# One transformer block: gate columns in place of gate rows, norms applied on ScalarE, a new order of stages

## The chip, the cores and the metric

The kernel runs on one core of one Trainium2 chip. The metric is the device time of one launch in microseconds (us), as the median of several runs. A core has five engines that run side by side and each work through their own instructions in order: TensorE (PE, matmuls), VectorE (DVE), ScalarE (ACT), GpSimd (POOL) and SyncE (SP), which here issues nearly all DMAs. They meet only through semaphores.

## The reference

The input `x` is 2 x 1024 x 512 in float32. A conditioning vector `c` (2 x 512) gives six modulation vectors of 512 per batch; two of them, `ga` and `gb`, are gates, clamped away from zero:

```python
mod = (_silu(c) @ wmod).reshape(2, 6, 1, -1)
sa, ca, ga, sb, cb, gb = ...
ga = (2 * (ga >= 0) - 1) * maximum(abs(ga), 0.25)      # gb the same
h = _layernorm(x) * (1 + ca) + sa
x = x + ga * attn(h)
h = _layernorm(x) * (1 + cb) + sb
x = x + gb * ffn(h)
```

`attn` is a convolution over time with 3 taps (512 to 3 x 128), projections to 16 heads of 64, causal attention within blocks of 128 positions, an output projection to 128 (`wo`) and one to 512 (`proj_w`). `ffn` is a base matmul 512 x 512 plus a low-rank part of rank 64 whose second factor is mixed from 16 experts, of which a softmax router picks two per position.

## The kernel before, in words

**Tiling.** The 2048 positions are worked in 8 chunks of 256 (index `j`), each as two blocks of 128 positions on the partitions (index `b`); `j` 0 to 3 is batch 0. Every float32 operand of the large matmuls is held as a high and a low half in float16, and a product is three matmuls (high x high, high x low, low x high; `PASSES`, `passes`). The halves are made in pairs of operations: ScalarE writes the high half, VectorE (sometimes GpSimd) subtracts and writes the low half. So nearly each result of TensorE passes ScalarE and then VectorE before TensorE can use it again and before its PSUM bank is free. There are three banks `C` (convolution, projections, `pr`, `lr`), one `W` (`pv`, `wo`), two `F` (ffn) and two `S` (scores).

**Order.** The text `SCHEDULE` (L64) lists stages as `name:j:n`. It is expanded to `ORDER` (L108), and each of the five engines loops over the same `ORDER` and issues its own part of each stage, with its waits. So the text fixes the order on every engine at once, but not the times: an engine is held only by its semaphores. `c:j:n` stands for the next `n` of the 108 convolution matmuls of chunk `j` (three thirds q, k, v, of 36), which are spread between other stages as filling.

**Stages that matter here.**
- `na` / `nb`: the first norm. VectorE computes mean and variance (L797), GpSimd forms 1/sqrt in a linked chain of six small operations (`root`, L538), VectorE then applies `(x - mean) * rstd` in place in `xa` (L805). `l2a` / `l2b` are the same for the second norm (L939, L949), from `xb` or `xa` to `xn2`.
- `hs` (L645, L810, L553): the high and low half of the normed chunk; SP turns them with two transposing DMAs into `hT` (L409), and issues the first loads behind them. `halo` (L557) copies the columns at chunk borders. `hs2`: the same for the second norm.
- `row` (L1040, L814): matmuls with the weights `wmod` give the modulation vectors as rows, each repeated over 32 partitions (`QUAD`); `row:0:0` is sa and ca, `row:0:2` is ga (made twice, for 64 partitions), `row:0:3` is sb, cb and gb. VectorE copies them out of PSUM; for `n` 2 and 3 it also clamps the gate, in four linked operations on whole rows of 512 (`clamp`, L777).
- `cols` (L1056, L825): TensorE transposes the rows of scale and shift to columns, VectorE stores them (`modT`, `shift`). The scale goes into the weights, in the splits `sp` (L639, L866); the shift goes through `vb` (convolution bias `cbias`), `fbias` and `lb`.
- `pick` (L1096, L852): one matmul against a selecting column spreads a gate row (or the ffn bias row) over all 128 partitions; VectorE copies it to `gaB`, `gbB` or `gbBB`.
- `pj` (L689, L871, L567): `proj_w` times the gate, split in halves: VectorE multiplies, ScalarE writes the high half, VectorE waits for it and writes the low half.
- `qk`, `v`, `s`, `m`, `e`, `nz`, `ph`, `pv`, `wo`, `pr`: projections, scores, row maxima, exponentials, normalization (GpSimd, L581), halves and transposes of the probabilities, values, output projections and residual. `lr`, `ro`, `rw`, `G`, `gh`, `fb`, `fl`, `gbb`, `xr`: the router, the ffn, its bias and the stores.

Of the kernel before, what the change touches and what calls it, by code (L numbers as in the profile page):

```python
# [42 lines left out]
def bass_adaln_block(nc, x, cw_in, pw_in, wo_in, pj_in, bsw_in, btw_in, ar_in, small_in, pb_in, bb_in, wmod_in,  # L43
# [26 lines left out]
        c:1:15 e:0:2 nz:0:2 c:1:3 cols:0:1 v:0:1 qk:1:0 pv:0:0 s:0:3 qk:1:5 m:0:3 ph:0:2 pick:0:2 qk:1:4 qk:1:1  # L70
        pv:0:1 c:1:3 sp:0:10 c:1:9 e:0:3 c:1:6 nz:0:3 c:1:12 pick:0:3 c:1:3 qk:1:6 v:0:3 c:1:3 hs:3:0 s:1:0 m:1:0
        halo:3:0 fbias:0:0 ph:0:3 qk:1:2 v:1:0 c:2:3 sp:0:7 c:2:6 e:1:0 c:2:3 nz:1:0 c:2:9 pick:0:4 pv:0:2 c:2:3
        qk:1:3 c:2:12 qk:1:7 s:1:1 m:1:1 ph:1:0 pv:0:3 pick:0:5 v:1:1 c:2:9 sp:0:9 c:2:6 e:1:1 c:2:3 nz:1:1 c:2:6
        qk:2:1 wo:0:0 c:2:3 s:1:2 c:2:6 m:1:2 c:2:3 pr:0:1 ph:1:1 pr:0:0 v:1:2 l2a:0:0 qk:2:5 qk:2:0 c:2:3 e:1:2
        c:2:6 nb:4:0 c:2:12 nz:1:2 c:2:3 l2b:0:0 c:2:9 pv:1:0 v:1:3 c:2:3 lb:0:0 s:1:3 hs2:0:0 hs:4:0 na:5:0 v:2:0
        v:2:1 m:1:3 qk:2:4 qk:2:3 xr:1:0 ph:1:2 qk:2:6 pv:1:1 lb:0:1 qk:2:2 lr:0:0 c:3:12 halo:4:0 c:3:3 e:1:3 c:3:3
        nz:1:3 c:3:6 s:2:0 ro:0:0 c:3:6 m:2:0 rw:0:0 ph:1:3 pv:1:2 qk:2:7 c:3:18 e:2:0 c:3:9 nb:5:0 c:3:6 nz:2:0
        c:3:6 ra:0:0 c:3:3 v:2:2 v:2:3 s:2:1 m:2:1 qk:3:1 ph:2:0 c:3:6 G:0:0 pv:1:3 c:3:3 sp:0:11 e:2:1 nz:2:1 c:3:9
# [1220 lines left out]
```

## Time and profile before

| | |
|---|---|
| median of 3 runs | 470.56 us (470.47 to 470.79) |
| the profiled execution's own time | 470.41 us |
| its span, first to last instruction | 468.4 us |
| mean granted TensorE clock | 0.984 |
| TensorE busy | 420.9 us (90%) |
| VectorE busy | 356.3 us (76%) |
| ScalarE busy | 302.0 us (64%) |
| GpSimd busy | 268.8 us (57%) |

All later times are of the profiled execution, counted from the start of its span. An engine's busy time leaves out its waits. In the rows further down, `L808` is line 808 of the kernel, `128x512 f16<-128x512 f32` is what an operation writes and reads (partitions x elements), `x16` a count, and a bracket `[6.92 <-DVE cv L886]` says how long the engine was idle before the instruction and whose end released it. A float32 matmul appears as two records in the trace.

### The profile page before, as it was taken

What the parts mean: (1) busy time and instruction counts of PE and PEld (TensorE: products, weight loads), DVE (VectorE), ACT (ScalarE), POOL (GpSimd) and SP (SyncE); (2) the same over time, 40 slices, a digit from 0 to 9 for tenths busy, and PEclk for the clock granted to TensorE, in tenths of its full rate; (3) what the DMA queues carried; (4) which work ended last, traced back from release to release, by engine and by line L of the source; (5) the groups of instructions that cost most, each with busy time, mean ns of one, the idle gap of its engine ahead of it and who ended that gap; (6) DMA issues with size and microseconds to landing.
All of it is one profiled execution on the core that took longest, in us unless ns stands there. A gap on an engine that the chain in (4) does not pass through costs nothing.

```text
span 468.4 us, 11145 instructions
## 1 busy us (share of the span) xinstructions
PE 420.9 (90%) x4170; PEld 270.2 (58%) x4170; DVE 356.3 (76%) x675; ACT 302.0 (64%) x974; POOL 268.8 (57%) x309
## 2 busy tenths in 40 slices
...
GB/s 318 235 397 388 207 206 46 59 123 47 80 147 113 158 133 202 143 84 115 181 72 157 163 49 145 111 139 117 156 115 46 47 136 90 153 142 45 136 80 77
DMA packets 144901, 65.09 MB, mean 139 GB/s; under 512 B 134704, under 2 KB 134960, under 8 KB 144464
## 3 DMA queue, kind: packets, MB, share of 16 engines
...
q8 instruction: 33, 0.54, 0.5%
q14 instruction: 20, 0.16, 0.1%
...
## 4 chain that ended last, share of the span: by engine, by line
PE 51%; DVE 16%; POOL 10%; DMA 9%; ACT 6%; issue 5%; SPq 2%; ACTq 0%; POOLq 0%; DVEq 0%
PE F L1024 15%; PE C L1133 12%; PE C L1024 10%; PE W L1024 3%; PE S L1179 3%; PE W L1196 3%; ACT prob L705 3%; DMA xa<-in_x_dram 3%; POOL prob L584 2%; DVE p L915 2%; DMA gT<-g 2%; PE S L1024 2%; DMA xb<-in_x_dram 2%; DVE nm L909 2%; DVE qk L895 2%
## 5 line engine op out<-in xcount | busy, mean ns | idle before, releaser
L1133 PE MATMUL C<-hT,cw 128*128 128x256 f16 x864 | 108.4, 277 | 13.0 <-DVE cv L886 6.9
L584 POOL TENSOR_TENSOR prob<-prob,rinv 128x1024 f32<-128x1024 f32 x32 | 62.4, 1948 | 73.7 <-DVE rinv L920 73.7
L1133 PEld LDWEIGHTS C<-hT,cw 128*128 128x128 f16 x864 | 83.0, 99 | 32.1 <-issue 7.4
L705 ACT ACTIVATE prob<-S,nms 128x128 f32<-128x128 f32 x256 | 89.9, 377 | 7.1 <-DVE p L915 6.0
L1024 PE MATMUL F<-btw,gT 128*128 128x512 f16 x336 | 74.8, 379 | 2.2 <-DMA gT<-g 2.1
L676 ACT ACTIVATE qk<-C,bqk 128x256 f16<-128x256 f32 x128 | 52.6, 479 | 14.2 <-PE C L1024 13.4
L895 DVE SCALAR_TENSOR_TENSOR qk<-C,bqk,qk 128x256 f16<-128x256 f32 x128 | 54.3, 474 | 4.6 <-ACT qk L676 4.6
L1024 PEld LDWEIGHTS F<-btw,gT 128*128 128x128 f16 x336 | 32.5, 98 | 40.7 <-DMA gT<-g 2.9
L705 ACT ACTIVATION_READ_ACCUMULATOR prob<-S,nms 128x1 f32 x256 | 55.5, 217 | 0.0
L1024 PE MATMUL C<-cv,pw 128*128 128x256 f16 x384 | 50.4, 273 | 2.4 <-DVE cv L886 1.9
L915 DVE SCALAR_TENSOR_TENSOR p<-prob,p 128x1024 f16<-128x1024 f32 x32 | 48.3, 1509 | 4.6 <-ACT p L714 4.3
L714 ACT ACTIVATE p<-prob 128x1024 f16<-128x1024 f32 x32 | 33.8, 1056 | 22.6 <-POOL prob L584 17.9
L909 DVE TENSOR_REDUCE nm<-S 128x4 f32<-128x512 f32 x64 | 41.0, 682 | 5.5 <-PE S L1179 5.4
L1024 PEld LDWEIGHTS C<-cv,pw 128*128 128x128 f16 x384 | 35.6, 98 | 13.1 <-DVE cv L886 3.4
L1024 PE MATMUL F<-bsw,h 128*128 128x512 f16 x168 | 38.4, 379 | 0.9 <-DVE ob L1014 0.9
L622 POOL TENSOR_TENSOR G<-cmb,lr 128x1024 f32<-128x1024 f32 x15 | 30.6, 2043 | 7.9 <-DVE cmb L998 4.0
L1196 PE MATMUL W<-pt,v 128*64 128x128 f16 x768 | 27.5, 221 | 4.4 <-issue 3.0
L1196 PEld LDWEIGHTS W<-pt,v 128*64 128x64 f16 x768 | 22.5, 110 | 14.3 <-issue 12.4
L1007 DVE TENSOR_TENSOR g<-G,g 128x1024 f16<-128x1024 f32 x15 | 24.2, 1613 | 6.9 <-ACT g L760 6.9
L540 POOL TENSOR_SCALAR rs<-mv 128x2 f32<-128x2 f32 x16 | 8.0, 500 | 34.7 <-DVE mv L803 18.4
L1179 PE MATMUL S<-qk 64*128 64x128 f16 x768 | 27.6, 220 | 0.0
L1024 PE MATMUL C<-pw,cv 128*128 128x512 f16 x96 | 25.0, 380 | 2.0 <-DVE cv L886 2.0
...
## 6 DMA issues: line engine op xcount, KB each, us to landing
...
wmb<-in_wmod_dram SPq DMA_DIRECT2D x1, 3072.0 KB, 19.1
...
```

The lines of the kernel that those rows point to most:

```text
L584: nc.gpsimd.tensor_tensor(prob[:], prob[:], rinv[:, i % 2].unsqueeze(2).broadcast_to([P, 8, P]), ALU.mult).then_inc(p_normal, 1)
L622: nc.gpsimd.tensor_tensor(G_of(i), cmb[:, n].unsqueeze(2).broadcast_to([P, E, R]), lr[:, n, 0:R].unsqueeze(1).broadcast_to([P, E, R]), ALU ...
L676: nc.scalar.activation(qk16[:, HI, c], C[k][:, a * CH:(a + 1) * CH], ACT.Identity, bias=bqk[:, c:c + 1]).then_inc(c_hi, 1)
L705: ins = nc.scalar.activation(prob[:, h], S[i % len(S)][h // 4][:, (h % 4) * P:(h % 4 + 1) * P], ACT.Exp, bias=nms[:, i % 2, h:h + 1], scal ...
L714: nc.scalar.activation(p16[:, HI], prob[:], ACT.Copy, scale=P_SCALE).then_inc(p_hi, 1)
L895: ins = nc.vector.scalar_tensor_tensor(out=qk16[:, LO, c], in0=C[k][:, a * CH:(a + 1) * CH], scalar=bqk[:, c:c + 1], in1=qk16[:, HI, c], o ...
L909: ins = nc.vector.tensor_reduce(nm[:, i % 2, 4 * h:4 * h + 4], S[i % len(S)][h][:].rearrange("p (h k) -> p h k", h=4), AX.X, ALU.max, nega ...
L915: nc.vector.scalar_tensor_tensor(out=p16[:, LO], in0=prob[:], scalar=P_SCALE, in1=p16[:, HI], op0=ALU.mult, op1=ALU.subtract).then_inc(p_l ...
L1024: ins = nc.tensor.matmul(dst, stat(a), mov(b), start=first and i == 0, stop=last and i == 2)
L1133: ins = nc.tensor.matmul(bank_c[:, 0:CH], cw[:, i, a, c, tap, :], hT[:, j % 2, b, c, OWN - 1 + tap:OWN - 1 + tap + CH], start=step == 0, s ...
L1179: ins = nc.tensor.matmul(S[i % len(S)][h][:, q * P:(q + 1) * P], qk16[of_head, hi, c, b * P:(b + 1) * P], qk16[of_head, lo, NC + c, b * P: ...
L1196: ins = nc.tensor.matmul(w_bank(stage)[DH * h:DH * (h + 1), q * P:(q + 1) * P], v16[:, j % 2, hi, b, of_head], pt16[:, i % 2, lo, 4 * h + ...
```

## The change

- The gate is clamped as columns. `cols` now also turns the gate rows (a new `cols:0:2` for ga, and `cols:0:1` takes 96 rows in place of 64), and `clamp` works on the 4 x 2 columns per partition: a copy and four linked operations on 128x8. `row:0:2` makes ga once instead of twice. A `pick` of a gate is now four matmuls of 128 columns against an identity, in place of one of 512.
- Both norms are applied by ScalarE, as `scale * x + bias` with scale = rstd and bias = -mean * rstd. VectorE gets a negation of the mean at the end of `na` and `l2a`, GpSimd one more multiplication in `root`; `na` and `l2a` wait for the former application to be done.
- `hs:1:0` is split by block into `hs:1:0` and `hs:1:1`, and `pj` into `pj` and `pk` (the low half).
- The identity matrix is 128x128 and the selecting columns are a view of it (two GpSimd operations fewer at the start).
- The whole order text is new, in its first stages and after them.

```diff
     SCHEDULE = """
-        na:0:0 sil:0:0 halo:0:0 nb:0:0 na:1:0 hs:0:0 row:0:0 nb:1:0 hs:1:0 cols:0:0 sp:0:0 c:0:6 sp:0:1 sp:0:2 c:0:9
-        halo:1:0 c:0:18 vb:0:0 na:2:0 vb:0:1 sp:0:3 c:0:9 sp:0:4 c:0:24 nb:2:0 c:0:3 qk:0:0 c:0:3 qk:0:1 sp:0:6
-        row:0:2 qk:0:4 qk:0:5 c:0:24 pick:0:0 pick:0:1 sp:0:5 c:0:12 qk:0:2 s:0:0 hs:2:0 m:0:0 qk:0:3 na:3:0 v:0:2
-        v:0:0 e:0:0 nz:0:0 row:0:3 c:1:3 halo:2:0 pj:0:0 c:1:6 s:0:1 m:0:1 ph:0:0 qk:0:6 c:1:3 qk:0:7 c:1:21 nb:3:0
+        na:0:0 sil:0:0 nb:0:0 na:1:0 hs:0:0 row:0:0 nb:1:0 cols:0:0 hs:1:0 sp:0:0 halo:0:0 halo:1:0 hs:1:1 c:0:33
+        sp:0:1 sp:0:2 vb:0:0 sp:0:3 vb:0:1 sp:0:4 c:0:15 na:2:0 sp:0:5 c:0:24 qk:0:3 qk:0:0 row:0:2 qk:0:1 cols:0:2
+        qk:0:4 qk:0:5 c:0:9 pick:0:0 pick:0:1 c:0:3 nb:2:0 c:0:6 pj:0:0 c:0:3 s:0:0 m:0:0 c:0:3 na:3:0 sp:0:6 qk:0:7
+        e:0:0 c:0:3 nz:0:0 c:0:9 qk:0:6 row:0:3 hs:2:0 s:0:1 halo:2:0 m:0:1 ph:0:0 v:0:1 qk:0:2 pk:0:0 v:0:3 e:0:1
+        pj:0:1 nz:0:1 cols:0:1 bias:0:0 pk:0:1 v:0:0 c:1:27 nb:3:0 c:1:9 s:0:2 c:1:3 m:0:2 c:1:6 ph:0:1 c:1:3 sp:0:7
...
-        pv:7:2 lr:6:0 fb:6:0 ro:6:0 pv:7:3 rw:6:0 G:6:0 wo:7:0 pr:7:0 pr:7:1 l2a:7:0 gh:6:0 fl:5:1 l2b:7:0 fb:6:1
-        hs2:7:0 G:6:1 gh:6:1 fl:6:0 lr:7:0 ro:7:0 rw:7:0 fb:7:0 G:7:0 fb:7:1 G:7:1 gh:7:0 fl:6:1 gbb:7:0 gh:7:1
-        fl:7:0 fl:7:1
+        l2a:7:0 gh:6:0 fl:5:1 fb:6:1 l2b:7:0 hs2:7:0 G:6:1 gh:6:1 gbb:6:0 gbb:7:0 fl:6:0 lr:7:0 ro:7:0 rw:7:0 G:7:0
+        fl:6:1 G:7:1 fb:7:0 fb:7:1 gh:7:0 gh:7:1 fl:7:0 fl:7:1
+        h_blocks = lambda j, n: (n,) if j == 1 else (0, 1)
 # SyncE, stage hs
-                    if j < 2:
-                        sp.dma_start(cw_raw[:, j + 1], cw_in[:, j + 1]).then_inc(ld[f"cw{j + 1}"], 16)
-                    if j == 1:
+                    if j + n < 2:
+                        sp.dma_start(cw_raw[:, j + n + 1], cw_in[:, j + n + 1]).then_inc(ld[f"cw{j + n + 1}"], 16)
+                    if j == 1 and n == 1:
 # GpSimd
-            def root(r, var, scale):
+            def root(r, var, scale, less):
...
-                return nc.gpsimd.tensor_tensor(r[:, 2], r[:, 2], r[:, 1], ALU.mult)
+                link(nc.gpsimd.tensor_tensor(r[:, 2], r[:, 2], r[:, 1], ALU.mult))
+                return nc.gpsimd.tensor_tensor(less, less, r[:, 2], ALU.mult)
 # ScalarE (l2b is the same, with xn2, xres(j), rs2, and the waits it had on VectorE)
+                elif s == "nb":
+                    act.wait_ge(rstd_ready, j + 1)
+                    for b in range(2):
+                        nc.scalar.activation(xa[:, j % 2, b], xa[:, j % 2, b], ACT.Identity, bias=rs[:, 3, b:b + 1],
+                                             scale=rs[:, 2, b:b + 1]).then_inc(xn_ready, 1)
 # VectorE (l2a likewise)
-            def clamp(rows, at, to):
-                g, a, b = rows[at:to, :], tmprow[at:to, 0], tmprow[at:to, 1]
+            def clamp(g, columns):
+
+                a, b = tmpcol[:, 0], tmpcol[:, 1]
+                link(nc.vector.tensor_copy(g, columns))
...
                 elif s == "na":
                     dve.wait_ge(ld_xa[j % 2], 16 * (j // 2 + 1))
+                    if j > 0:
+                        dve.wait_ge(xn_ready, 2 * j)
...
-                    ins.then_inc(var_ready, 1)
-                elif s == "nb":
-                    dve.wait_ge(rstd_ready, j + 1)
-                    for b in range(2):
-                        nc.vector.tensor_scalar(xa[:, j % 2, b], xa[:, j % 2, b], mv[:, b, 0:1], rs[:, 2, b:b + 1],
-                                                ALU.subtract, ALU.mult).then_inc(xn_ready, 1)
+                    link(ins)
+                    nc.vector.tensor_scalar(rs[:, 3], mv[:, :, 0], -1.0, None, ALU.mult).then_inc(var_ready, 1)
...
-                    copied = nc.vector.tensor_copy(dst[:], m_bank(stage)[0:dst.shape[0], :])
-                    if n == 0:
-                        copied.then_inc(m_done, 1)
-                    else:
-                        link(copied)
-                        clamp(dst, 0 if n == 2 else 2 * QUAD, dst.shape[0]).then_inc(m_done, 1)
+                    nc.vector.tensor_copy(dst[:], m_bank(stage)[0:dst.shape[0], :]).then_inc(m_done, 1)
                 elif s == "cols":
...
+                    if n > 0:
+                        ins = clamp(gate[:, 2 - n], at[:, rows - 1, :, 0:NB])
+                    ins.then_inc(m_done, 1)
...
                     nc.vector.tensor_tensor(pjt[:], pjw_raw[:], gaB[:, n], ALU.mult).then_inc(pj_prod, 1)
+                elif s == "pk":
                     dve.wait_ge(pj_hi, n + 1)
 # TensorE
-                        for i, m in enumerate([(0, 1), (), (2, 2), (0, 1, 2)][n]):
+                        for i, m in enumerate([(0, 1), (), (2,), (0, 1, 2)][n]):
...
+                    rows = (row_ab, row_cdg, ga_row)[n]
+                    r = rows.shape[0]
                     for k in range(DC):
-                        ins = nc.tensor.transpose(m_bank(stage)[:, 2 * k * QUAD:2 * (k + 1) * QUAD],
-                                                  rows[0:2 * QUAD, k * P:(k + 1) * P], ident[:])
+                        ins = nc.tensor.transpose(m_bank(stage)[:, k * r:(k + 1) * r], rows[:, k * P:(k + 1) * P],
+                                                  ident[0:r, 0:r])
...
-                    of = (("row", 2), ("row", 3), ("fbias", 0))[n // 2]
+                    of, b = (("cols", 2), ("cols", 1), ("fbias", 0))[n // 2], n % 2
...
+                    if n < 4:
+
+                        for k in range(DC):
+                            ins = nc.tensor.matmul(m_bank(stage)[:, k * P:(k + 1) * P],
+                                                   gate[:, n // 2, k, b:b + 1].broadcast_to([P, P]), ident[:],
+                                                   start=True, stop=True)
```

## Rows read from the trace of the kernel before

**Rows 1.** The page: busy time of each engine, its share of the span, instructions.

```profile
PE 420.9 (90%) x4170; PEld 270.2 (58%) x4170; DVE 356.3 (76%) x675; ACT 302.0 (64%) x974; POOL 268.8 (57%) x309
```

**Rows 2.** Stretches: from:to, length, busy PE PEld DVE ACT POOL (instructions), clock, DMA, GB/s.

```profile
60.00:67.20 7.20, 0.36 (x4) 0.07 (x1) 6.50 (x13) 6.33 (x24) 0.00 (x0) 0.77 0.70 230
67.20:72.00 4.80, 4.73 (x47) 3.29 (x48) 3.65 (x7) 2.81 (x4) 4.36 (x3) 0.63 0.18 34
100.00:145.00 45.00, 39.99 (x479) 30.97 (x478) 39.17 (x79) 35.19 (x118) 22.23 (x32) 1.00 0.41 81
145.00:335.00 190.00, 189.72 (x1977) 126.35 (x1974) 154.13 (x280) 144.17 (x483) 125.27 (x127) 1.00 0.62 131
335.00:384.00 49.00, 42.27 (x497) 29.06 (x497) 39.23 (x78) 36.35 (x127) 32.86 (x31) 1.00 0.49 99
```

**Rows 3.** TensorE in order of time: start us, us, instruction [idle before <-releaser].

```profile
67.27 1.46 PE L1133 MATMUL C<-hT,cw 128*128 128x256 f16 x6 [6.92 <-DVE cv L886]
```

**Rows 4.** VectorE in order of time, in and before the long wait.

```profile
54.10 2.17 DVE L779 SCALAR_TENSOR_TENSOR tmprow<-row_cdg 32x512 f32<-32x512 f32 x1
...
58.20 1.64 DVE L782 SCALAR_TENSOR_TENSOR row_cdg<-tmprow 32x512 f32<-32x512 f32 x1
...
65.76 1.00 DVE L808 TENSOR_SCALAR xa<-xa,mv,rs 128x512 f32<-128x512 f32 x2
...
66.74 0.48 DVE L886 SCALAR_TENSOR_TENSOR cv<-C,cbias,cv 128x256 f16<-128x256 f32 x1
```

**Rows 5.** Groups by line and shape: xcount | busy us, mean ns | idle before.

```profile
L958 DVE TENSOR_SCALAR xn<-xb,mv,rs 128x512 f32<-128x512 f32 x12 | 11.2, 974 | 1.0 <-POOL rs L545 1.0
...
L808 DVE TENSOR_SCALAR xa<-xa,mv,rs 128x512 f32<-128x512 f32 x16 | 10.5, 700 | 1.4 <-POOL rs L545 1.4
...
L920 DVE RECIPROCAL rinv<-rsum 128x8 f32<-128x8 f32 x32 | 6.4, 199 | 21.6 <-ACT prob L705 21.4
...
L650 ACT ACTIVATE h<-xa 128x512 f16<-128x512 f32 x16 | 9.4, 641 | 11.2 <-DVE xa L808 5.8 <-DMA hT<-h 5.4
...
L644 ACT ACTIVATE bsw<-raw,modT 128x512 f16<-128x512 f32 x4 | 2.6, 706 | 0.0
...
L545 POOL TENSOR_TENSOR rs<-rs 128x2 f32<-128x2 f32 x16 | 4.3, 266 | 1.3
```

**Rows 6.** VectorE in order of time, 120 to 125: one applied norm.

```profile
121.71 2.58 DVE L958 TENSOR_SCALAR xn<-xb,mv,rs 128x512 f32<-128x512 f32 x2
```

**Rows 7.** TensorE in order of time: gate rows, picks of a gate, nearest shape.

```profile
35.62 3.63 PE L1053 MATMUL F<-wma,silw 128*32 128x512 f32 x16
...
43.22 1.13 PE L1107 MATMUL S<-ga_row,sel 32*128 32x512 f32 x4
...
49.53 3.63 PE L1053 MATMUL F<-wmb,silw 128*32 128x512 f32 x24
...
78.84 1.12 PE L1107 MATMUL F<-row_cdg,sel 32*128 32x512 f32 x2
...
122.98 1.02 PE L1093 MATMUL F<-ar_raw,shift 128*128 128x80 f32 x8
```

**Rows 8.** TensorE in order of time: first convolution matmuls, first projection.

```profile
19.73 5.33 PE L1133 MATMUL C<-hT,cw 128*128 128x256 f16 x33 [4.70 <-DVE cw L869]
...
33.88 0.83 PE L1024 MATMUL C<-cv,pw 128*128 128x256 f16 x6 [0.64 <-DVE cv L886]
```

**Rows 9.** The last load of gate weights: issue, then time to landing.

```profile
L434 SPq DMA_DIRECT2D wmb<-in_wmod_dram x1: 1347/1347/1347, 28.8 to 28.8; - x1
...
DMA to landing us min/median/max: 19.1/19.1/19.1
```

**Rows 10.** VectorE and TensorE in order of time, near the end.

```profile
432.69 2.98 DVE L985 TENSOR_TENSOR h<-xn,h 128x512 f16<-128x512 f32 x2
...
439.90 1.02 PE L1024 MATMUL C<-arw,h 128*128 128x80 f16 x24 [0.92 <-issue]
```

**Rows 11.** Waits of ScalarE: us in total, times, longest.

```profile
ACT p L714 <- POOL prob L584: 17.9, 11, 4.0
```

More of the change, by code:

```diff
@@ L70, in bass_adaln_block @@
[L70 to L78, printed above, removed]
-        ra:0:1 c:3:9 gbb:0:0 fb:0:0 gh:0:0 c:3:3 G:0:1 wo:1:0 c:3:3 s:2:2 m:2:2 ph:2:1 c:3:3 qk:3:5 pv:2:0 fb:0:1
@@ new lines, in bass_adaln_block @@
+        s:1:2 c:2:3 m:1:2 c:2:6 sp:0:9 nb:5:0 ph:1:1 c:2:6 wo:0:0 c:2:6 qk:2:5 qk:2:0 pick:0:4 e:1:2 pr:0:0 pr:0:1
+        nz:1:2 v:2:0 pick:0:5 v:2:2 pv:1:0 hs:4:0 s:1:3 m:1:3 lb:0:0 ph:1:2 l2a:0:0 qk:2:4 v:2:3 qk:2:1 e:1:3 nz:1:3
+        pv:1:1 lb:0:1 halo:4:0 qk:2:7 qk:2:2 c:3:3 xr:1:0 c:3:3 s:2:0 l2b:0:0 m:2:0 c:3:6 ph:1:3 qk:2:3 c:3:3
+        hs2:0:0 c:3:9 e:2:0 c:3:3 nz:2:0 c:3:15 pv:1:2 c:3:15 gbb:0:0 s:2:1 c:3:3 m:2:1 c:3:3 sp:0:10 pv:1:3 c:3:6
+        ph:2:0 qk:2:6 c:3:3 na:6:0 v:2:1 e:2:1 nz:2:1 wo:1:0 lr:0:0 qk:3:5 ro:0:0 s:2:2 pr:1:1 pr:1:0 m:2:2 c:3:3
@@ new lines, in bass_adaln_block @@
+        c:4:3 gh:1:0 qk:4:1 c:4:6 xr:2:0 c:4:3 m:3:2 ph:3:1 fb:1:1 gbb:1:0 qk:4:0 c:4:3 pr:2:1 c:4:3 e:3:2 c:4:12
+        nz:3:2 c:4:12 pv:3:0 c:4:6 hs:6:0 nb:7:0 G:1:1 pr:2:0 s:3:3 m:3:3 qk:4:7 ph:3:2 pv:3:1 l2a:2:0 qk:4:4
+        halo:6:0 qk:4:5 e:3:3 nz:3:3 gh:1:1 fl:1:0 qk:4:2 v:4:1 c:5:9 s:4:0 m:4:0 c:5:3 l2b:2:0 pv:3:2 c:5:9 hs2:2:0
+        c:5:3 ph:3:3 qk:4:6 c:5:3 qk:4:3 e:4:0 c:5:3 nz:4:0 c:5:3 gbb:2:0 ra:0:3 c:5:3 fl:1:1 s:4:1 m:4:1 lr:2:0
+        ph:4:0 v:4:0 v:4:3 pv:3:3 e:4:1 c:5:15 ro:2:0 c:5:18 nz:4:1 c:5:3 v:4:2 rw:2:0 s:4:2 m:4:2 ph:4:1 wo:3:0
@@ new lines, in bass_adaln_block @@
+        xr:4:0 pr:4:0 nz:5:2 ra:0:4 pr:4:1 gbb:3:0 v:5:2 v:5:1 s:5:3 m:5:3 pv:5:0 ph:5:2 l2a:4:0 qk:6:2 c:6:3 gh:3:1
+        sp:0:15 c:6:6 e:5:3 nz:5:3 fl:3:0 qk:6:3 l2b:4:0 c:6:15 ra:0:5 pv:5:1 s:6:0 m:6:0 hs2:4:0 ph:5:3 c:6:9
+        qk:6:6 c:6:3 sp:0:16 e:6:0 nz:6:0 fl:3:1 qk:6:7 pv:5:2 s:6:1 m:6:1 ph:6:0 v:6:2 gbb:4:0 v:6:1 pv:5:3 c:7:18
+        e:6:1 c:7:6 lr:4:0 c:7:3 ro:4:0 nz:6:1 c:7:6 xr:5:0 c:7:3 v:6:0 s:6:2 m:6:2 ph:6:1 wo:5:0 rw:4:0 qk:7:1
+        qk:7:0 c:7:9 e:6:2 c:7:18 pr:5:0 nz:6:2 G:4:0 v:6:3 c:7:9 s:6:3 m:6:3 pv:6:0 pr:5:1 xr:6:0 ph:6:2 l2a:5:0
```

132 lines of the change are left out of this document (61 added, 71 removed).

## The prediction

> **What bounds the kernel now.** I read the page's busy table first: TensorE is busy 420.9 of 468.4 us, so at most 47.5 us of the span is not matmul time; VectorE has 356.3, ScalarE 302.0, GpSimd 268.8 [rows 1]. The reader should take from it that TensorE is the resource, and that only what TensorE waits for, or is made to do, moves the end.
>
> Next the stretches [rows 2]. From 145 to 335 us TensorE is busy 189.7 of 190: nothing done on another engine can be gained there, only lost. Three places are open: 60 to 67.2 (busy 0.36 of 7.2, VectorE 6.5), 100 to 145 (5.0 idle, VectorE 39.2 of 45) and 335 to 384 (6.7 idle, VectorE 39.2 of 49). Behind the first hole the granted clock is 0.63 for 4.8 us, while everywhere else in these rows it is 1.00: a hole is paid once as idle time and again as slow matmuls.
>
> Then TensorE in order of time: the hole is one wait of 6.92 us for VectorE's low half of the convolved block [rows 3]. VectorE in order of time says why it was late: the four operations of `clamp` on the 32x512 gate row run from 54.10 to 59.84, and a norm application of 1.00 us is still ahead of the `cv` operation at 66.74 [rows 4]. VectorE was never idle for long there; it had a queue, and the gate's clamp and the norm are in it.
>
> **The change, part by part.** The sum is made against the profiled execution: span 468.4 us, own time 470.41, so 2.0 us lie around the span. That execution is 0.15 us under the median of 470.56.
>
> *Clamp on columns.* The clamp of the 32x512 rows, 5.7 us [rows 4], becomes a copy and four linked operations on 8 elements per partition. VectorE's reciprocal on 8 elements is 0.20 [rows 5], so five of them are 1.0. That takes 4.7 us out of the queue before `cv`. The norm application there (1.0) goes too. Relief is 5.7 against a wait of 6.9; the leftover is 1.2. `pj` is also split in two (`pj`, `pk`), so VectorE no longer stands inside it, but the order is new, and in-order engines find some other wait. I leave 1.5 us: minus 5.4. Bounds: minus 6.9 (nothing left) and 0 (something else as late as `cv` was).
>
> *The clock behind it.* 4.73 busy us at 0.63 are 1.75 us of loss [rows 2]. With a wait of 1.5 instead of 6.9 I take minus 1.6; bounds minus 1.75 and 0.
>
> *Norms on ScalarE.* There are 32 applications. 28 of them cost VectorE 11.2 + 10.5 us, 0.78 each [rows 5]; all 32, 24.8. ScalarE's nearest rows on 128x512 from SBUF are 0.641 (plain copy) and 0.706 (one per-partition operand) [rows 5]; this one has two, scale and bias, so I go on by the difference: 0.77, bounds 0.64 and 0.97 (VectorE's own dearer group). 32 x 0.77 = 24.6 us for ScalarE, which goes from 302.0 to 327, 70% of the span: not a bound by itself. VectorE goes down by 24.8, less 16 negations of 0.20, less the clamps.
> The Trainium skill ("ScalarE: Activation LUTs", What ACT_TABLE_LOAD costs) says an activation costs 186 ns plus 0.833 ns per element, and 93 ns more for each per-partition operand. The two rows agree within 0.03 us (0.613 and 0.706 by the rule). By it this one is 0.80, an estimate, and ScalarE ends 1 us busier; the sum stays.
>
> Where does the relief reach the end? In 100 to 145 one application alone holds VectorE 2.58 us [rows 6] just ahead of the work that TensorE wants. I take a third of the 5.0 idle us: minus 1.7, bounds minus 5.0 and plus 1.6 (two applications on ScalarE, 2 x 0.77, in front of an eviction). In 335 to 384 the idle time has more owners (late loads of the residual, softmax chains); minus 1.0, bounds minus 6.7 and plus 3. In 145 to 335 it is worth nothing.
>
> *Added links.* Each norm gets a negation on VectorE (0.20) and a multiply on GpSimd (0.27 [rows 5]) in its chain, and the next `na` or `l2a` waits until ScalarE has read the statistics. Fifteen of the sixteen chains have matmuls of other blocks beside them. The last second norm does not: its h2 opens the last router matmul, before which TensorE already waits 0.92 [rows 10]. The chain gets 0.20 + 0.27 for links; the first of its two applications and the first copy behind it are now one queue on ScalarE, while VectorE, which held a subtraction pair of 2.98 us there [rows 10], is freer. I take plus 0.6, bounds minus 0.9 and plus 1.9. The final order (`fl:6:1` ahead of `fb:7`) moves TensorE's work within a fixed sum: 0.
>
> *TensorE's own work.* The gate row `row:0:2` issues 8 matmuls in place of 16. One would book half of 3.63 us; but the row for 24 such matmuls also lasts 3.63 [rows 7]: the 32-column groups run side by side, and the duration is that of 8 in sequence. So 0 (bound minus 1.8). `cols:0:2` adds four transposes, and `cols:0:1` makes its four wider: plus 0.4 together (bounds 0.1 and 0.9: they are smaller than the 8 in 1.02). A gate pick becomes 4 matmuls in float32, 8 records. The nearest shape, 8 records of 128x80, takes 1.02 [rows 7]; I take 1.1. The first two picks took 1.13 as a pair, so each adds 0.55; the other two took 1.12 each and add nothing. Together plus 1.5, bounds minus 1.7 and plus 2.6.
>
> *First stages.* The first convolution matmul starts at 19.73, waiting for VectorE's cw split, and the first projection at 33.88 [rows 8]. `cols:0:0` and the split now stand ahead of the second block's h, which gains; but `na:1` waits for ScalarE's two applications, which are dearer (2 x 0.77 against 1.00 for both on VectorE [rows 4]), so the first transposes go out over 1 us later; and the third load of cw now leaves SP behind one transpose. `vb:0:1` no longer stands behind `na:2` on VectorE, but it stands behind `sp:0:3`. I find gains and losses of under 1 us each and take 0, bounds minus 1.5 and plus 1.5. The big load of gate weights lands at 28.8 + 19.1 = 47.9 [rows 9], and its matmuls begin at 49.53 [rows 7]. TensorE gets 1.5 us of new work before them, so this wait stays hidden; if the order were to reach it earlier, it costs up to 1.5. On SP, pw's loads go behind the second block's last transpose; the cw load in front of it keeps the queue filled.
>
> Sum: minus 5.4, minus 1.6, minus 1.7, minus 1.0, plus 1.5, plus 0.6 = minus 7.6. Span 460.8, time 462.8.
>
> **The rivals.** *A: the hole moves.* TensorE is in order, and before the wait sat also a softmax chain of GpSimd and ScalarE. If VectorE is early, this or a load is late instead, and of the 7.0 us (hole and clock) only 1.5 come back: 462.8 + 5.5 = 468.3. For it: ScalarE is busy 6.33 of the 7.2 us of the hole [rows 2]. Against: the releaser named is VectorE [rows 3], whose queue has the 5.7 us in it.
>
> *B: more holes close.* The relief is spread over the whole run. Of the 5.0 + 6.7 = 11.7 idle us in the two open stretches it then closes 9.4 in place of my 2.7, 6.7 more: 462.8 minus 6.7 = 456.1. For it: VectorE is the fullest engine behind TensorE in both [rows 2]. Against: idle time in the third stretch also has loads behind it, which nothing here speeds up. The Trainium skill ("GPSIMD Engine Reference", 1. Specifications) says GpSimd shares its SBUF interface with VectorE and is disturbed by VectorE's two-port modes and its operations with two SBUF inputs. The trace agrees in kind: applications that take 1.00 a pair in [rows 4] take 2.58 a pair in [rows 6]. By the rule the move frees GpSimd as well, which is B; it does not free the subtractions, which have two SBUF inputs.
>
> *C: slower, ScalarE stands in front of GpSimd.* `nb` and `l2b` are now blocking waits in ScalarE's in-order queue, for a chain of seven small GpSimd operations that themselves stand behind `nz` or `xr`. Behind them on ScalarE wait the evictions of C and W, and for those TensorE. Price: 0.8 us (one application of 0.77) lost on TensorE at 14 of the 16 norms, most in the full stretch: plus 11.2, time 474.0. It decides from 7.6/14 = 0.54 us a norm. For it: TensorE has no slack from 145 to 335. Against: ScalarE already waits 17.9 us in 11 waits for GpSimd's `prob`, up to 4.0 [rows 11], and TensorE stays full there; ScalarE is idle for a third of the time.
>
> **How the numbers follow.** Forecast 0.53, A 0.17, B 0.16, C 0.14. A measurement of this kernel can tell about 0.2% (0.9 us) from no change. The forecast and B are faster; A is, by 2.2 us, in most of its range; so faster 0.83, same 0.04, slower 0.13. Range: 456.0 takes in B; above, it goes through A to 470.0, and leaves out C. With the bounds of the single terms (about 4 us either way) the forecast case lies within 458.5 to 467.
>
> **What would show it.** Right: no TensorE wait above 2 us between 50 and 75; granted clock 1.00 in all of it; VectorE's busy time near 328, ScalarE's near 327; ScalarE's norm at 0.7 to 0.8 us; the gate pick near 1.1 us for 8 records; `row:0:2` still about 3.6 us; first projection at 33 to 35 us. Wrong: a wait over 3 us in the same place with another releaser (A); idle time left in the stretches that answer to 100 to 145 and 335 to 384: about 9 us would be mine, about 2 B; TensorE's idle time between 145 and 335 above 5 us, ended by evictions behind a norm on ScalarE (C).

## The result, and the profile after

The changed kernel took 487.28 us (median of 6 runs, 484.41 to 488.30) against 470.51 us (468.72 to 471.95) of the kernel before beside it: a ratio of 1.0335, 95% interval 1.0300 to 1.0369. It is slower. Here and below a median counts every execution, while a ratio leaves out slow executions, such as those over 1.5% above the fastest of the same kernel (none in this comparison, two or three of twelve in three later ones). The forecast was 462.8, its range ended at 470.0; the price named for rival C (474.0) was passed too. The profiled execution took 485.85 us with a span of 483.8, so it is 15.4 us longer than the one before.

The page's busy table, to be held against [rows 1]:

```profile
PE 429.3 (89%) x4190; PEld 277.4 (57%) x4190; DVE 333.7 (69%) x661; ACT 322.5 (67%) x1006; POOL 269.1 (56%) x323
```

Work went where the forecast sent it: VectorE fell from 356.3 to 333.7 (I had said near 328), ScalarE rose to 322.5 (near 327). Only TensorE, which sets the end, went up, by 8.4 us, of which about 1.5 was to be new work. Most of the rest goes with the clock: the mean granted clock fell from 0.984 to 0.965. The groups by line and shape of the kernel after (count | busy us, mean ns of one | idle before) show that the single durations were right: a norm application on ScalarE at 0.81 to 0.84 us (0.77 forecast), a gate pick at 1.95 to 2.1 us for two (1.1 each), the 8 records of the gate row at 3.6 like the 16 before [rows 7].

```profile
L648 ACT ACTIVATE xa<-xa,rs 128x512 f32<-128x512 f32 x16 | 12.2, 823 | 9.8 <-POOL rs L545 9.8
L659 ACT ACTIVATE xn<-xb,rs 128x512 f32<-128x512 f32 x12 | 9.3, 836 | 0.4 <-POOL rs L545 0.4
...
L1061 PE MATMUL F<-wma,silw 128*32 128x512 f32 x8 | 3.6, 592 | 1.7 <-issue 1.7
L1111 PE MATMUL F<-ident,gate 128*128 128x128 f32 x16 | 2.1, 275 | 0.0
```

So the durations are not what was wrong; the time is in waits and in the clock. By stretches, first of the kernel before, then of the one after (columns as in [rows 2]):

```profile
60.00:80.00 20.00, 12.89 (x142) 8.54 (x140) 18.12 (x32) 15.78 (x51) 9.30 (x10) 0.83 0.52 118
300.00:350.00 50.00, 48.75 (x501) 31.68 (x500) 38.15 (x73) 35.79 (x120) 30.70 (x29) 1.00 0.58 123
```

```profile
60.00:80.00 20.00, 15.71 (x138) 11.40 (x138) 12.74 (x28) 12.70 (x44) 2.17 (x3) 0.83 0.87 205
100.00:145.00 45.00, 40.97 (x489) 31.01 (x488) 37.71 (x67) 39.76 (x120) 27.20 (x29) 1.00 0.44 87
145.00:300.00 155.00, 152.40 (x1614) 102.56 (x1613) 119.33 (x241) 123.40 (x405) 103.98 (x122) 1.00 0.64 134
300.00:335.00 35.00, 27.04 (x209) 15.87 (x206) 20.01 (x34) 18.16 (x56) 15.47 (x15) 0.80 0.41 90
300.00:350.00 50.00, 41.70 (x377) 25.27 (x375) 31.05 (x54) 29.89 (x92) 23.69 (x21) 0.86 0.44 98
335.00:384.00 49.00, 48.09 (x556) 33.78 (x554) 37.65 (x72) 40.08 (x142) 34.23 (x34) 1.00 0.48 95
```

The reader should see three things. The hole of [rows 2] shrank (idle in 60 to 80: 7.1 before, 4.3 after), but the clock in it did not recover. The open stretch 100 to 145 gained 1.0 us, not 1.7. And 300 to 350, nearly full before, now has 8.3 us idle and a clock of 0.86: 377 matmul records instead of 501. Against that, 335 to 384, where 6.7 us were idle before [rows 2], now has only 0.9. Over 300 to 384 together the idle time is 8.9 us against 6.8, so more is lost there to the clock: 27.0 busy us at 0.80 are 5.4 us of loss, where the kernel before ran at 1.00.

TensorE in order of time after the change, its waits in these stretches and near the end:

```profile
61.10 0.81 PE L1032 MATMUL C<-pw,cv 128*128 128x512 f16 x3 [1.60 <-DVE v L919]
68.32 2.36 PE L1142 MATMUL C<-hT,cw 128*128 128x256 f16 x12 [2.06 <-POOL hT L533]
80.23 0.41 PE L1180 MATMUL S<-mask,ident 64*64 64x512 bf16 x4 [1.36 <-ACT prob L721]
...
312.37 2.74 PE L1032 MATMUL C<-pjw,att 128*128 128x512 f16 x6 [4.08 <-DVE att L946]
320.27 1.44 PE L1032 MATMUL C<-pw,cv 128*128 128x512 f16 x3 [3.88 <-DVE xb L952]
...
454.39 7.04 PE L1032 MATMUL F<-btw,gT 128*128 128x512 f16 x24 [4.23 <-DMA gT<-g]
461.26 5.34 PE L1032 MATMUL S<-bsw,h 128*128 128x512 f16 x24
469.28 10.53 PE L1032 MATMUL S<-btw,gT 128*128 128x512 f16 x48 [2.68 <-DMA gT<-g]
```

Each has an owner in the new order. At 312, ScalarE waited 8.2 us in stage `sp:0:14` (it overwrites `bsw`, whose last reader `fb:3:0` stands further on), so ScalarE's evictions behind it were late:

```profile
ACT bsw L644 <- PE F L1032: 8.2, 1, 8.2
```

At 320 the residual came late: SyncE had stored the old block at 297.25, but reloads only in `xr` or behind a transpose of p, and the next of these came at 311.94.

```profile
297.25 0.36 SPq L489 DMA_DIRECT2D out_dram<-xb  x1
303.06 1.86 SPq L475 DMA_TRANSPOSE gT<-g  x1
311.94 1.76 SPq L467 DMA_TRANSPOSE pt<-p  x1
313.76 1.15 SPq L399 DMA_DIRECT2D xb<-in_x_dram  x1
```

At the end `fl:6:1` stands ahead of `fb:7`. Its matmuls wait for their own transposes, VectorE's `ob` for it waits 7.28 us for them, and the activation product of the last block is behind `ob`; its transposes go out only at 464.87. TensorE ends its last other work at 466.60 and waits 2.68 us for them. VectorE and then SyncE:

```profile
461.46 0.69 DVE L1022 TENSOR_TENSOR ob<-F,gbB 128x512 f32<-128x512 f32 x1 [7.28 <-PE F L1032]
462.07 1.22 DVE L1015 TENSOR_TENSOR g<-G,g 128x1024 f16<-128x1024 f32 x1
```

```profile
451.76 13.01 SPq L489 DMA_DIRECT2D out_dram<-xa  x2
464.87 1.88 SPq L475 DMA_TRANSPOSE gT<-g  x1
```

Followed by its matmuls, the kernel after is 8.3 us behind at `wo:7:0` and 15.4 us behind at the last matmuls (`fl:7:1`): 7.1 us are lost in the tail alone. Both kernels have the same 210 matmul records left at `wo:7:0`; the kernel after is idle 4.1 us longer among them and busy 3.0 us longer.

### The profile page after: what moved, and what is told of

It reads as the page before. It is cut to its first block, busy times and chain, and to the rows that moved or that the text cites. A ratio compares the mean times of both kernels' runs of the same rounds, so it can differ in the third digit from the quotient of the medians.

```text
span 483.8 us, 11222 instructions
## 1 busy us (share of the span) xinstructions
PE 429.3 (89%) x4190; PEld 277.4 (57%) x4190; DVE 333.7 (69%) x661; ACT 322.5 (67%) x1006; POOL 269.1 (56%) x323
## 4 chain that ended last, share of the span: by engine, by line
PE 57%; DVE 12%; DMA 9%; ACT 7%; issue 6%; POOL 6%; SPq 3%; ACTq 0%; POOLq 0%; DVEq 0%
PE F L1032 17%; PE C L1032 11%; PE C L1142 11%; DMA pt<-p 4%; PE W L1032 4%; PE W L1205 4%; PE S L1188 3%; ACT prob L721 3%; SPq L420 2%; PE S L1032 2%; DVE p L931 2%; DMA gT<-g 2%; PE S L1180 1%; DVE st L820 1%; DVE btw L884 1%
## 5 line engine op out<-in xcount | busy, mean ns | idle before, releaser
L1142 PE MATMUL C<-hT,cw 128*128 128x256 f16 x864 | 110.7, 281 | 6.3 <-DVE cw L884 4.2
L1142 PEld LDWEIGHTS C<-hT,cw 128*128 128x128 f16 x864 | 84.4, 101 | 23.5 <-issue 4.4
L584 POOL TENSOR_TENSOR prob<-prob,rinv 128x1024 f32<-128x1024 f32 x32 | 60.7, 1896 | 41.0 <-DVE rinv L936 41.0
L1032 PE MATMUL F<-btw,gT 128*128 128x512 f16 x336 | 76.5, 386 | 5.8 <-DMA gT<-g 5.8
L931 DVE SCALAR_TENSOR_TENSOR p<-prob,p 128x1024 f16<-128x1024 f32 x32 | 49.6, 1550 | 7.9 <-ACT p L730 7.5
L925 DVE TENSOR_REDUCE nm<-S 128x4 f32<-128x512 f32 x64 | 40.9, 681 | 5.4 <-PE S L1188 5.3
L739 ACT ACTIVATE oT<-W 128x512 f16<-128x512 f32 x32 | 19.6, 611 | 19.1 <-PE W L1205 18.9
L1032 PE MATMUL C<-pw,cv 128*128 128x512 f16 x96 | 26.5, 395 | 5.7 <-DVE xb L952 3.9
L1205 PEld LDWEIGHTS W<-pt,v 128*64 128x64 f16 x768 | 23.0, 112 | 11.2 <-issue 9.9
L579 POOL TENSOR_TENSOR xb<-xb,gaPB 128x512 f32<-128x512 f32 x12 | 19.9, 1682 | 14.9 <-DMA xb<-in_x_dram 14.8
```

The source lines that it names most:

```text
L579: nc.gpsimd.tensor_tensor(xres(j)[:, b], xres(j)[:, b], gaPB[:, batch(j)], ALU.add).then_inc(xr_biased, 1)
L584: nc.gpsimd.tensor_tensor(prob[:], prob[:], rinv[:, i % 2].unsqueeze(2).broadcast_to([P, 8, P]), ALU.mult).then_inc(p_normal, 1)
L925: ins = nc.vector.tensor_reduce(nm[:, i % 2, 4 * h:4 * h + 4], S[i % len(S)][h][:].rearrange("p (h k) -> p h k", h=4), AX.X, ALU.max, nega ...
L931: nc.vector.scalar_tensor_tensor(out=p16[:, LO], in0=prob[:], scalar=P_SCALE, in1=p16[:, HI], op0=ALU.mult, op1=ALU.subtract).then_inc(p_l ...
L1032: ins = nc.tensor.matmul(dst, stat(a), mov(b), start=first and i == 0, stop=last and i == 2)
L1142: ins = nc.tensor.matmul(bank_c[:, 0:CH], cw[:, i, a, c, tap, :], hT[:, j % 2, b, c, OWN - 1 + tap:OWN - 1 + tap + CH], start=step == 0, s ...
```

## The experiments

"New order" is that of the change, "old order" that of the kernel before. All ratios are to the kernel before on the same chip; its medians there were 471.1 to 471.6.

**The new operations in the old order.** T1 is that the operations gain what was forecast and the order loses it, T2 that the operations lose by themselves.

```diff
 # old order text, with only the stages that the new code needs
+ hs:1:1 behind hs:1:0;  cols:0:2 behind qk:0:4;  pk:0:0, pk:0:1 behind pj:0:0, pj:0:1
```

> All new operations (gates as columns, norms on ScalarE, pk split from pj), but the order text of the kernel before, with the new stages put in where their work stood. Theory 1 (the operations are worth what the prediction said, and the loss sits in a few places of the new order): 462 to 467 us, no TensorE wait above 2.5 us between 50 and 75 us. Theory 2 (a norm on ScalarE is a blocking wait in an in-order queue and costs wherever it stands): 476 us or more, with waits of ScalarE for GpSimd's chain in front of late evictions.

481.98 us, 1.0229 (1.0177 to 1.0281). The operations cost 2.3% in an order written for others; the new order adds the rest. T1 fell, and T2 alone does not reach 487. The intervals of the two ratios do not overlap, so the new order does add to the loss.

**Two stages of the new order, one by one and together.**

```diff
-gh:3:0 sp:0:14 ph:5:1 wo:4:0 qk:6:4 qk:6:0 fb:3:0 G:3:1 e:5:2   # sp14_later
+gh:3:0 ph:5:1 wo:4:0 qk:6:4 qk:6:0 fb:3:0 G:3:1 e:5:2 sp:0:14
-rw:7:0 G:7:0 fl:6:1 G:7:1 fb:7:0 fb:7:1 gh:7:0 gh:7:1   # tail_old
+rw:7:0 fb:7:0 G:7:0 fb:7:1 G:7:1 gh:7:0 fl:6:1 gh:7:1
```

> The changed kernel with one stage moved in the order text: sp:0:14, the split of the second batch's base weights, from in front of ph:5:1 to behind fb:3:0 and e:5:2. ScalarE waits in it for TensorE's fb:3:0 (8.2 us in the trace), which stands behind ph:5:1 and wo:4:0 on TensorE. Theory 1: the waits of 4.08 and 3.88 us at 312 and 320 go, and most of the 5.8 us that the lower clock costs there; 474 to 477 us. Theory 2 (norms on ScalarE): the wait is a symptom, another takes its place, 484 us or more.

480.28 us, 1.0198 (1.0160 to 1.0235): 7.0 us less than the change. The wait on `att` is gone, that on `xb` stays (3.70).

> The changed kernel with the last stages in the former order: fb:7 ahead of fl:6:1 on TensorE, and fl:6:1 behind gh:7:0 on VectorE and SyncE. Theory 1: the wait of 4.23 us at 454.4 and the transposes held behind the store go; 479 to 482 us. Theory 2: the end is set by when the last second norm is applied, 485 us or more.

481.02 us, 1.0180 (1.0144 to 1.0216): 6.3 less.

> Both moves in one kernel. Theory 1: the two add up, 466 to 471 us, at or under the kernel before. Theory 2: 480 us or more.

475.44 us, 1.0084 (1.0052 to 1.0116): together 11.8 less, near the sum of the two (13.3). I had asked for 466 to 471, so more was wrong than these two.

**Which new operation costs in the old order.** T3 is that the norms on ScalarE cost and the gates gain, T4 the reverse.

```diff
 # gates_old_order: new_ops_old_order, but stages nb and l2b apply the norm on VectorE again
 # norms_old_order: the kernel before, but nb and l2b as in the change
 # both keep the negation and the seventh operation of root
```

> The former order with the gates as columns and pk split off, but both norms applied by VectorE as before (the added negation and the seventh GpSimd operation are left in). Theory 3 (the norms on ScalarE cost, the gates as columns gain): the hole at 60 us closes as in new_ops_old_order, the waits after 350 us do not grow; 467 to 471 us. Theory 4 (the gates' new chain, row, columns, clamp, pick, is what costs): 476 us or more.

478.44 us, 1.0173 (1.0124 to 1.0223).

> The kernel before with one thing changed: both norms are applied by ScalarE (with the negation, the seventh GpSimd operation and the waits). Gates as rows, order as before. Theory 3: slower, 476 to 481 us: 1.1 us at the start, then evictions that stand behind the norm on ScalarE, 6 us of it after 350 us. Theory 4: 468 to 472 us.

480.04 us, 1.0208 (1.0160 to 1.0257). Either part costs by itself, and both together (1.0229) hardly more than one: neither theory held, and the parts do not add up. One reason can be read from the traces: both kernels hold the two links that the change adds to each norm's chain, and `gates_old_order` has them though it does not use them. VectorE and TensorE in it:

```profile
15.15 1.00 DVE L813 TENSOR_SCALAR xa<-xa,mv,rs 128x512 f32<-128x512 f32 x2 [0.92 <-POOL rs L545]
...
20.36 6.54 PE L1141 MATMUL C<-hT,cw 128*128 128x256 f16 x33 [5.54 <-DVE cw L883]
```

In the kernel before, VectorE applies this norm at 14.38 without a wait, and the same 33 matmuls start at 19.73 and take 5.33 us [rows 8]. So 1.8 us are lost there before any gate is touched: 0.6 to the later start, which the links explain, and 1.2 to the clock (granted 0.57 from 20 to 27, against 0.79), which they need not: `norms_late` below starts at the same time and takes 5.40. A kernel with the links alone was not run, so what they cost further on is open.

Around the hole the gates do what they were forecast to do: the wait at the hole falls to 2.81 us, and TensorE, 3.3 us late before it, is 0.8 early behind it. That lead is lost again at waits which were there before. One of them in the kernel before and then with the gates changed:

```profile
102.32 0.86 PE L1196 MATMUL W<-pt,v 128*64 128x128 f16 x24 [1.57 <-issue]
103.11 1.13 PE L1107 MATMUL F<-fb_rows,selsum 128*128 128x512 f32 x2
104.08 0.81 PE L1024 MATMUL C<-pw,cv 128*128 128x512 f16 x3
```

```profile
103.34 0.86 PE L1204 MATMUL W<-pt,v 128*64 128x128 f16 x24 [2.08 <-issue]
104.13 1.67 PE L1114 MATMUL F<-fb_rows,selsum 128*128 128x512 f32 x2
105.59 1.48 PE L1031 MATMUL C<-pw,cv 128*128 128x512 f16 x3
```

The wait is 0.5 us longer, and the same matmuls behind it then run at the lower clock (1.67 for 1.13, 1.48 for 0.81; the granted clock from 102.3 to 107 is 0.74 against 1.00). From 102.3 to `wo:0:0` the lag goes from 1.0 to 2.7.

With the norms on ScalarE, VectorE's waits for ScalarE grew (total us, times, longest), before and after that edit:

```profile
DVE qk L895 <- ACT qk L676: 4.6, 11, 0.8
DVE v L903 <- ACT v L687: 4.2, 5, 1.1
DVE cv L886 <- ACT cv L661: 2.0, 4, 0.7
```

```profile
DVE qk L910 <- ACT qk L693: 9.9, 10, 2.8
DVE cv L901 <- ACT cv L678: 9.8, 5, 4.0
DVE v L918 <- ACT v L704: 8.3, 7, 4.1
```

One place of it, ScalarE, then VectorE, then TensorE: a norm of two blocks, their two copies and the norm of two other blocks in a row, and only then the first half of an eviction, for whose second half VectorE has stood idle.

```profile
251.02 1.55 ACT L660 ACTIVATE xn<-xb,rs 128x512 f32<-128x512 f32 x2
252.43 1.17 ACT L755 ACTIVATE h<-xn 128x512 f16<-128x512 f32 x2
253.47 1.53 ACT L649 ACTIVATE xa<-xa,rs 128x512 f32<-128x512 f32 x2
254.88 0.61 ACT L704 ACTIVATE v<-C 128x512 f16<-128x512 f32 x1
...
255.52 0.69 DVE L918 TENSOR_TENSOR v<-C,v 128x512 f16<-128x512 f32 x1 [4.12 <-ACT v L704]
...
257.14 0.82 PE L1031 MATMUL C<-cv,pw 128*128 128x256 f16 x6 [1.56 <-DVE cv L901]
```

**Norms of the first two chunks back on VectorE**, in the old order. (The expectation counts the first norms only; of the second norms two waited as well, 1.5 and 6.1 us, the latter for the last one.)

```diff
-                elif s == "nb":                 # ScalarE, from norms_old_order
+                elif s == "nb" and j >= 2:      # and the old code on VectorE for j < 2
```

> The kernel before with the norms on ScalarE (480.0 us), but those of chunks 0 and 1 on VectorE as before. ScalarE waited 11.1 us for rs in its first three norms and not at all in the other eleven. Theory: the ScalarE queue is held only at the start, there it costs 1.3 us at the first convolution and what follows from the lower clock, so the time falls by 1 to 3 us, to 477 to 479, and the other 6 to 8 us come from the longer ScalarE work in all later chunks. Rival: the delay of the start is what shifts everything behind it; then 471 to 474.

481.38 us, 1.0195 (1.0153 to 1.0237): no gain. The first convolution starts at 20.37 instead of 21.01, as in `gates_old_order`, which has the same links; but that gain does not last, and TensorE reaches `wo:0:0` at 112.64 instead of 112.69. Where ScalarE applies the first norms is not what costs.

**Three norms one eviction later**, in the old order.

```diff
-l2b:0:0 c:2:9 pv:1:0 v:1:3      nb:7:0 c:5:6 v:4:1      l2b:5:0 e:7:0 c:7:12
+c:2:9 pv:1:0 v:1:3 l2b:0:0      c:5:6 v:4:1 nb:7:0      e:7:0 c:7:12 l2b:5:0
```

> The kernel before with the norms on ScalarE (480.0 us), and three of the fourteen norms one eviction later in the written order: l2b:0:0 behind pv:1:0 and v:1:3, nb:7:0 behind v:4:1, l2b:5:0 behind e:7:0. In that kernel ScalarE did xn, h and xa at 251.0 to 255.0 back to back, v's upper half stood behind them, VectorE waited 4.12 us for it and TensorE 1.56 us. Theory: the norms cost because they stand ahead of evictions that ScalarE does the first half of and VectorE the second; then these three waits fall (1.51 at 131, 1.56 at 257, 2.21 at 385, by about 1.0 to 1.5 us each), and the time to 475.5 to 478. Rival: it is the 21 us of added ScalarE work as such, wherever it stands; then the waits only move and the time stays at 479 to 481.

478.30 us, 1.0153 (1.0128 to 1.0179), against 1.0208 (1.0160 to 1.0257) without the move: a gain that the intervals, which overlap, do not make sure. In the trace one of the three paid: ahead of `wo:6:0` the wait fell from 2.21 to 1.08 and 1.4 us of lag went. The other two only changed their wait (1.51 and 0.59 from 131 on became 1.17 and 0.93; 1.56 at 257 became 1.32, with the lag unchanged). Place may explain a part; most of the 9 us stays unexplained by a single cause.

**Loads and transposes on SyncE, in the new order.** First `hs:2:0` ahead of `row:0:3` (which issues three 1 MB loads), on top of sp14_and_tail:

```diff
-qk:0:6 row:0:3 hs:2:0
+qk:0:6 hs:2:0 row:0:3
```

> sp14_and_tail with a third move: hs:2:0 in front of row:0:3, so that SyncE issues the transposes of chunk 2 ahead of the 3 MB of ffn weights (in the changed kernel they take 8.5 us behind these, against 2.6 before). If the wait of 1.9 us for the halo at 68 us and part of the 2.9 us at 80 us come from that: 471 to 474 us. If they come from ScalarE's queue: no change, 475 to 476 us.

478.67 us, 1.0144 (1.0076 to 1.0211): no gain; it is 3.2 us above sp14_and_tail, but the intervals overlap. The wait for the halo went, and a wait of 6.20 us for ScalarE's `prob` came at 82. ScalarE in turn had waited 7.2 us for the transposes of p, which were now the ones behind the loads. SyncE's transposes (duration ns min/median/max, first and last start; then issue to landing): hT in the change, p in this kernel, where the first of the two, at 63.5, is the one behind the loads and has the maxima.

```profile
L420 SPq DMA_TRANSPOSE hT<-h x2: 3539/4231/4923, 58.2 to 61.8; - x2
...
DMA to landing us min/median/max: 6.9/8.3/9.6
```

```profile
L466 SPq DMA_TRANSPOSE pt<-p x2: 1919/5736/9552, 63.5 to 77.5; - x2
...
DMA to landing us min/median/max: 4.3/7.9/11.5
```

Then each load behind one transpose:

```diff
-# stage row:0:3: bs, bt half 0, bt half 1
+# stage ph, behind its transpose: ph:0:0 bs; ph:0:1 bt half 0; ph:0:2 bt half 1
```

> The kernel with sp:0:14 later, the old tail and hs:2 ahead of row:0:3; on top of it SyncE issues the three 1 MB loads (bs, bt in two halves) one behind each of the first three p transposes, instead of all three ahead of the first. Theory: a transpose that is issued behind these loads takes 8 to 11 us to land instead of 3 to 4 (hT of chunk 2 where row:0:3 stands first, pt of the first unit where hs:2 stands first), and the TensorE wait only moves from one to the other (1.85 us at 67.8 and 2.93 at 79.8 in the one, 6.20 at 82.2 in the other). Then both waits go: the transposes land within 4.5 us, the wait at 82 falls below 2 us and the time is 471 to 474. Rival: ScalarE is late there for its own work (qk, bsw split); then the wait stays above 5 us and the time is 476 to 479.

472.13 us, 1.0009 (0.9984 to 1.0034), 3.3 under sp14_and_tail and 6.5 under three_moves. hT lands again as it did before the change:

```profile
L419 SPq DMA_TRANSPOSE hT<-h x2: 1309/1685/2061, 58.1 to 60.2; - x2
...
DMA to landing us min/median/max: 3.1/3.2/3.4
```

The price of a transpose behind loads is shown, and the gain over sp14_and_tail is clear of both intervals. That the wait on `prob` would fall below 2 us was a miss: it is 4.26 at 77.5, since TensorE now gets there sooner.

**Norms back on VectorE in the new order** (three_moves with `nb` and `l2b` on VectorE):

> three_moves with both norms applied by VectorE again. Theory 3: 465 to 469 us. Theory 4, or if the new order needs the norms on ScalarE: 473 us or more, as VectorE gets its 25 us back in an order planned without them.

487.61 us, 1.0336 (1.0276 to 1.0396): 9 us worse than with them on ScalarE. The same move costs 2.1% in the old order (with the links; on top of the gates it is 0.6%, within the noise) and gives 1.9% in the new, which was written for norms on ScalarE. What an operation costs is a property of it and the order together.

**The wait at 314: the reload, or the split.**

```diff
+                # SyncE, stage gh, behind its transpose (reload_early, on sp14_and_tail;
+                # all_moves: on loads_spread)
+                    if reload:
+                        load_again(reload.pop())
```

> The kernel with sp:0:14 later and the old tail; on top of it SyncE also reloads the residual in the gh stages (it does so otherwise only behind a p transpose or in xr), so the load no longer stands behind ph:5:1. Theory: the 3.78 us wait of TensorE at 314 (on xb, VectorE's, which waits for that load) goes, and the time falls by 3 to 5 us, to 470.5 to 472.5. Rival: another wait (on VectorE's own work) stands right behind it and less than 1 us is won: 474.5 to 476.

473.34 us, 1.0029 (1.0002 to 1.0056), 2.1 under sp14_and_tail, but the wait is still 3.86 us: the rival was right about it. The profiled run is no shorter (span 473.3 against 473.2) and the intervals of the two ratios overlap, so the 2.1 may be noise.

> Both of these edits on the new order: sp:0:14 later, old tail, hs:2 ahead of row:0:3 with the three loads spread, residual reloaded in gh. Theory: they add up, 466 to 470, at or under the kernel before. Rival: the time given back by the late work of ScalarE and VectorE in the first two chunks holds it at 472 or more, so the new order is no better than the old even without its misplaced stages.

472.20 us, 0.9992 (0.9964 to 1.0020): it does not add up with loads_spread, and its wait at 314 is still 3.70.

```diff
# split_behind_pr: on loads_spread; split_and_reload: the same move, and the reload in gh
-sp:0:14 xr:4:0 pr:4:0 nz:5:2 ra:0:4 pr:4:1
+xr:4:0 pr:4:0 nz:5:2 pr:4:1 sp:0:14 ra:0:4
```

> loads_spread (472.1 us) with sp:0:14, the two bsw splits, behind pr:4:1 instead of ahead of xr:4:0. In reload_early the TensorE wait at 316 stayed at 3.86 us though the reload was issued 0.8 us sooner: VectorE did the bsw split (3.01 us) right ahead of the xb eviction that TensorE waits for, and ScalarE's half of it stands ahead of its own evictions. Theory: the split's place holds that wait, it falls below 2 us and the time is 468 to 470.5. Rival: the DMA of the residual alone ends it (GpSimd waits 5.8 us for it); then the wait stays above 3 us and the time at 471.5 to 473.

474.25 us, 1.0036 (1.0008 to 1.0065); wait 3.98, ended by the load (GpSimd waits 6.0 us for it). No gain alone.

> The same with the residual reloaded in the gh stages too. Theory: both the split and the load hold the wait at 314, so only this kernel loses it wholly: 467 to 469.5, below the kernel before. Rival: the load does not matter; then as split_behind_pr within 1 us.

470.10 us, 0.9945 (0.9920 to 0.9970). Only with both does the wait fall to 1.45:

```profile
310.66 0.81 PE L1035 MATMUL C<-pw,cv 128*128 128x512 f16 x3 [1.45 <-DVE xb L955]
```

Two late things side by side held it, each hiding the other. A wait of 1.61 us for VectorE's `v` now follows, but TensorE needs 44.4 us from `wo:4:0` to `wo:5:0`, against 47.0 in loads_spread, 46.4 with only the reload added (all_moves) and 47.4 with only the split moved (split_behind_pr). This is the fastest version measured, with all of the change's operations: 3.5% under the change by the medians, 3.8% by the ratios. Whether it beats the kernel before is not sure. The ratio says 0.55%, but it leaves out three of the twelve executions, and the medians of all (470.10 against 471.41) are only 0.3% apart, while its times run from 466.07 to 474.18.

**How far a single trace carries.** The last matmuls of three of these kernels, which have the same order from `wo:7:0` on (sp14_and_tail, loads_spread, split_and_reload):

```profile
458.68 10.53 PE L1031 MATMUL S<-btw,gT 128*128 128x512 f16 x48 [2.98 <-DMA gT<-g]
...
456.71 11.96 PE L1033 MATMUL S<-btw,gT 128*128 128x512 f16 x48 [3.01 <-DMA gT<-g]
...
454.66 13.46 PE L1035 MATMUL S<-btw,gT 128*128 128x512 f16 x48 [3.01 <-DMA gT<-g]
```

The same matmuls behind the same wait differ by up to 2.9 us. From `wo:7:0` to the end all three are idle 5.6 us and busy 40.9, 43.2 and 44.7. So a difference of 2 or 3 us between two single traces can be the clock alone. The profiled executions of loads_spread (474.71) and split_and_reload (474.18) are indeed 2.6 and 4.1 us above their medians.

## Why the prediction was wrong, step by step

*The whole order.* The failed step is the one that charges the new order nothing: "The final order (`fl:6:1` ahead of `fb:7`) moves TensorE's work within a fixed sum: 0", and no term at all for the places of `sp:0:14` and `row:0:3`. With `sp:0:14`, `fl:6:1`, `hs:2:0`, the three loads and the reload in other places, and no operation changed, the ratio went from 1.0335 to 0.9945. That is 3.9 points, 17 us by the medians and 18 by the ratios, where 24.5 lie between forecast and result. Not all of it is damage that the change did: the reload's place is as in the kernel before, and the loads spread behind transposes are new to both kernels. Whether these two would also gain in the old order was not tried. A fixed sum of matmuls is no fixed time: transposes, evictions and loads pass from engine to engine in that order.

*Hole and clock: minus 5.4 and minus 1.6.* The clock in the hole was misread: it is not 1.00 everywhere else in [rows 2], but 0.77 from 60 to 67.2. The releaser was VectorE's queue as said: with the gates alone in the old order the wait fell from 6.92 to 2.81. In the change three waits of 1.60, 2.06 and 1.36 took its place, idle time in 60 to 80 fell by 2.8 us, and the clock gained nothing: 0.83 in 60 to 80 and 0.86 in 50 to 75 in both kernels, where the sign named was 1.00. Of the 7.0 us, 2.8 came back, nearer to A's 1.5 than to the forecast. The second of the three is a transpose behind loads, a cause that comes near the rival A's "this or a load is late instead".

*100 to 145: minus 1.7.* 1.0 was gained. (The row of 2.58 us that stood for one application counts two.) *335 to 384: minus 1.0.* The idle time there fell by 5.8 us, but 7.9 us of new idle time stand in 300 to 335, from `sp:0:14` and the reload, with 5.4 us of clock: over 300 to 384 the change lost.

*Norms at 0.77.* The size was right within 0.07 us, the busy totals within 6 us; where they stand was wrong to ignore. I treated ScalarE's third of idle time as cover; but it evicts the first half of each pair whose second half is VectorE's, and its order is fixed. Rival C had the right engine, the right sign and, in the old order, about the right size (9 us against 11.2), but not the right mechanism. Half of what would have shown it did appear: 10.6 us are idle between 145 and 335. But 8.0 of them stand behind 300 and are ended by `att` and `xb`, behind the split and the reload, and ScalarE's waits on `rs` are few (9.8 us in 2 for xa, 9.0 in 3 for xn in the kernel after). In the old order VectorE's longer waits for ScalarE point to ScalarE's own work ahead of the pairs; moving it paid in one place of three, so this is not shown for the rest.

*TensorE's own work: plus 1.5, tail plus 0.6.* The picks, and the gate row at 3.60, were right (the 8 and 16 "matmuls" of the text are records). The tail cost 7.1, of which the old tail order gave back 6.3.

*First stages: 0.* The first projection came at 34.02, in the range named. But TensorE waits 1.71 us ahead of the gate row (the group L1061 above), where there was no wait before, and the matmuls of the big gate load start at 51.77 instead of 49.53.

*What B would have shown*, about 2 us idle in 100 to 145 and 335 to 384 together, did not appear: 4.9 are left (4.0 and 0.9), about half of what the forecast expected, yet the time went to other places. GpSimd, which B expected to be freed, is busy 269.1 us, as before (268.8).

*Open.* Why either half of the change costs 7 to 9 us in the old order has no single cause that I could take out; the traces show a start that the links delay by 0.6 us, many waits of 0.5 to 1.5 us longer than before and slow matmuls behind several, and one of three moves tried there paid. In the new order 470.1 is still 7 above the forecast.
